# Attention and feed-forward layer on one core: GpSimd takes the residual addition, and four orders of work are changed

## What is computed

```python
attn_out = softmax(q @ k.T / sqrt(32) + mask) @ v @ Wo.T + bo    # 16 heads of 32, keys 0..2047
a = layernorm(x + attn_out) * gamma + beta
x = layernorm(x + a)                              # first output, "x1"
xh = x @ H                                        # Hadamard, 512 x 512
scale = max(|xh|, axis=-1) / 7
xq = clip(round(xh / scale), -8, 7) * scale       # 4 bits
wq = ternary(weight)
x = layernorm(x + xq @ wq.T)                      # the output
```

## Time and profile before

| | |
|---|---|
| time, 3 runs | 4688.91 us median, 4688.58 to 4694.65 |
| profiled execution | 4689.32 us, span 4687.4 us |
| busy share of the span | PE 97%, DVE 71%, ACT 54%, POOL 78% |
| first token stage | 1113.8 to 1273.5 us: 159.7 us, of which PE is busy 143.9, DVE 117.6, POOL 88.2 |
| last token stage | 4539.0 to 4687.4 us |

### The profile page before, as it was taken

One profiled execution on the slowest core, in us unless ns is written; L12 is line 12 of the kernel. 1 busy time (PEld: TensorE's weight loads), 2 busy tenths in 40 slices (PEclk: granted clock), 3 DMA queues, 4 the chain that ended last, 5 costly groups with the idle time before them and its releaser, 6 DMA issues.

```text
span 4687.4 us, 65375 instructions
## 1 busy us (share of the span) xinstructions
PE 4528.7 (97%) x24114; PEld 2416.8 (52%) x24152; DVE 3331.9 (71%) x5886; ACT 2528.7 (54%) x4890; POOL 3642.7 (78%) x1215
## 2 busy tenths in 40 slices
PE   7999999999899999999999999999989999999987
PEld 4545555554555555555454555555545555555434
DVE  5777777677777677777777777776786777777728
ACT  1555555554555555555455555555545555555545
POOL 1788888887488888888758888888865888888885
PEclk9999999999999999999999999999999999999998
DMA  8213333334421333333341233233434123332112
GB/s 174 73 41 73 71 65 71 70 66 111 110 66 41 65 72 70 73 73 74 107 108 42 57 73 69 65 77 62 94 96 111 42 57 62 75 66 62 30 54 75
DMA packets 245776, 344.89 MB, mean 74 GB/s; under 512 B 14801, under 2 KB 100561, under 8 KB 245458
## 3 DMA queue, kind: packets, MB, share of 16 engines
q1 hardware_dynamic: 243282, 339.68, 32.5%
q10 hardware_dynamic: 2176, 1.05, 0.2%
HBM read 205.33 MB, written 33.55 MB: 51 GB/s over the span
## 4 chain that ended last, share of the span: by engine, by line
PE 67%; POOL 20%; DVE 7%; ACT 2%; issue 2%; DMA 2%; SPq 0%; DVEq 0%; POOLq 0%; ACTq 0%
POOL acc L1139 20%; PE ps_m L529 16%; PE ps_s L544 15%; PE ps_o L574 15%; PE ps_z L516 5%; PE ps_z L549 4%; PE ps_z L484 4%; PE ps_m L490 4%; ACT prob L793 1%; PE ps_s L484 1%; PE ps_s L490 1%; PE ps_s L628 1%; DVE prob L1036 1%; DVE ps_m L1026 1%; DVE ps_s L1010 1%
## 5 line engine op out<-in xcount | busy, mean ns | idle before, releaser
L1139 POOL TENSOR_TENSOR acc<-acc,prob 128x2048 f32<-128x2048 f32 x624 | 2859.0, 4582 | 139.3 <-ACT prob L793 65.1
L950 DVE TENSOR_REDUCE umax<-ps_m 128x1 f32<-128x512 f32 x4071 | 2484.6, 683 | 654.3 <-PE ps_m L529 654.3
L793 ACT ACTIVATE prob<-ps_s 128x512 f32<-128x512 f32 x4096 | 2063.6, 625 | 866.8 <-PE ps_s L544 850.5
L529 PE MATMUL ps_m<-kst,qst 97*128 97x512 f32 x4071 | 1722.5, 424 | 8.7 <-DVE umax L950 5.4
L544 PE MATMUL ps_s<-qst,kst 99*128 99x512 f32 x4096 | 1597.2, 411 | 23.6 <-ACT prob L793 18.8
L529 PEld LDWEIGHTS ps_m<-kst,qst 97*128 97x128 f32 x4071 | 768.7, 189 | 579.7 <-DVE umax L950 366.7
L544 PEld LDWEIGHTS ps_s<-qst,kst 99*128 99x128 f32 x4096 | 776.8, 190 | 391.8 <-ACT prob L793 245.2
L574 PE MATMUL ps_o<-prob,vst 128*32 128x512 f32 x8192 | 975.1, 599 | 0.0
L1139 POOL TENSOR_TENSOR acc<-prob 128x2048 f32<-128x2048 f32 x64 | 291.2, 4550 | 322.6 <-ACT prob L793 322.6
L574 PEld LDWEIGHTS ps_o<-prob,vst 128*32 128x32 f32 x8192 | 227.7, 109 | 480.2 <-issue 292.2
L962 DVE RECIPROCAL zinv<-ps_z 128x512 f32<-128x512 f32 x64 | 214.9, 3358 | 272.7 <-PE ps_z L549 272.7
(11 more groups left out here) (123 smaller groups left out, 2558.4 us busy)
## 6 DMA issues: line engine op xcount, KB each, us to landing
xk<-in_xT_dram SPq DMA_DIRECT2D x66, 1024.0 KB, 8.7
xq<-in_xT_dram SPq DMA_DIRECT2D x65, 1024.0 KB, 5.9
kst<-hi SPq DMA_DIRECT2D x128, 256.0 KB, 6.8
qst<-hi SPq DMA_DIRECT2D x128, 256.0 KB, 5.6
wq<-in_wT_dram SPq DMA_DIRECT2D x65, 256.0 KB, 6.2
kst<-lo SPq DMA_DIRECT2D x64, 256.0 KB, 5.6
qst<-lo SPq DMA_DIRECT2D x64, 256.0 KB, 6.8
ctxT_dram<-obuf SPq DMA_DIRECT2D x64, 256.0 KB, 2.4
```

Of the source, the lines that this page charges most:

```text
L529: nc.tensor.matmul(first_banks[u % len(first_banks)] if first else ps_m[:, u % NMB, :], qst[k % 2][0:RSTACK, h, qt * P:(qt + 1) * P], kst[ ...
L793: nc.scalar.activation(prob[:, c % NPB, h, :], ps_s[:, (i * HG * NKC + HG * c + h) % NSB, :], ACT.Exp, scale=SCALE).then_inc(ex, 1)
L950: nc.vector.tensor_reduce(umax[:, m, kb:kb + 1], bank, AX.X, ALU.max).then_inc(mred, 1)
L1139: nc.gpsimd.tensor_tensor(acc[:], a, prob[:, c % NPB], ALU.add).then_inc(padd, 1)
```

## The change

1. **Residual on POOL.** DVE writes the scaled product straight to `tO` in SBUF, and L1032 goes. POOL adds the rows x1 (`residual`) after the butterfly's first half and ahead of its second. The statistics of the second norm are taken ahead of those of the third. PE's waits on `c_fo` become waits on `c_fs`.
2. **Centring in halves.** L1010 becomes two instructions of 256 columns; the first stands ahead of the norms' chain, where DVE waits for ACT's square root.
3. **Keys earlier in the tail.** PE makes a quarter's keys ahead of the step's transposes; ACT and DVE take them in the same step, ahead of rounding and of the scaled product; SP stacks them a step earlier.
4. **Start.** The quarters of stage 1 use slots (0, 1, 1, 0).
5. **Last block.** SP stacks the queries' high parts ahead of the load of the last weights.

The slots of the start, and SP's order in the last block:

```diff
+SECOND = (0, 1, 1, 0)
...
-                    if i == NBLK - 1:
-                        load_last_projection(n)
                     wait_alone(sp, sc, (n + 1) * (HG * NKC), passed)
                     if not (last and i >= NBLK - 2):
                         queries(n + 2, i + 2)
+                    if i == NBLK - 1:
+                        load_last_projection(n)
+                    if not (last and i >= NBLK - 2):
                         low_queries(n + 2, i + 2)
```

PE's program of a token stage, behind the projection of tile s+1 (the call of `keys_of` at the step's end goes):

```diff
+                    t = s - KEY_STEP
+                    if not last and 0 <= t < NQB:
...
+                        keys_of(stage, t, ps_wo[(NT - 3) % 3])
                     t = s - 3
```

ACT's program of a token stage:

```diff
-                    t = s - KEY_STEP - 1
+                    t = s - KEY_STEP
                     if not last and 0 <= t < NQB:
...
                         keys_of(stage, NG + 1, t, ps_wo[(NT - 3) % 3])
+                    t = s - KEY_STEP - 1
+                    if not last and 0 <= t < NQB:
+                        values_of(bb * NG + (NG + 1), NG + 1, t, ps_wo[(NT - 2) % 3])
                     t = s - 3
```

DVE's program of a token stage; `centre(y, half)` is the instruction of L1010 on one half of the columns:

```diff
+                        if 0 <= y < NT:
+                            dve.wait_ge(c_mv, bb * (3 * NT) + moments_by(s))
+                            centre(y, 0)
                         dve.wait_ge(c_sd, bb * (STEPS - 1) + s)
...
                     if 0 <= y < NT:
-                        nc.vector.scalar_tensor_tensor(out=ps_wo[y % 3], in0=ps_wo[y % 3], scalar=mv[:, LN1, 0:1], in1=gam,
-                                                       op0=ALU.subtract, op1=ALU.mult).then_inc(c_ng, 1)
+                        centre(y, 1)
...
-                    k = s - KEY_STEP - 1
+                    k = s - KEY_STEP
...
                     if 0 <= f < NT:
-                        dve.wait_ge(c_ffn, bb * NT + (f + 1))
-                        nc.vector.scalar_tensor_tensor(out=ps_f[f % 2], in0=ps_f[f % 2], scalar=qsc[:, f % 2, 1:2],
-                                                       in1=wscale[:], op0=ALU.mult, op1=ALU.mult).then_inc(c_fs, 1)
-                    if 0 <= f < NT:
...
-                        dve.wait_ge(c_fs, bb * NT + (f + 1))
-                        nc.vector.tensor_tensor(tO[f % NST], ps_f[f % 2], tY[f % 4], ALU.add).then_inc(c_fo, 1)
+                        dve.wait_ge(c_ffn, bb * NT + (f + 1))
+                        nc.vector.scalar_tensor_tensor(out=tO[f % NST], in0=ps_f[f % 2], scalar=qsc[:, f % 2, 1:2],
+                                                       in1=wscale[:], op0=ALU.mult, op1=ALU.mult).then_inc(c_fs, 1)
```

POOL's program of a token stage:

```diff
+                def residual(b, f):
+                    if 0 <= f < NT:
+                        pool.wait_ge(c_fs, b * NT + (f + 1))
+                        nc.gpsimd.tensor_tensor(tO[f % NST], tO[f % NST], tY[f % 4], ALU.add).then_inc(c_fo, 1)
+
...
                     nc.gpsimd.tensor_tensor(tB[:, half:], src[:, 0:half], src[:, half:], ALU.subtract).then_inc(c_bf, 1)
+                    residual(b, t - 2)
                     sv = tB.rearrange("p (a b n) -> p a b n", a=2, b=2)
```

More of the change, by code:

```diff
@@ L294, in stack, with keys_quarter @@
                     sp.dma_start(dst[HD * r:HD * r + HD].bitcast(F32), part.bitcast(F32)).then_inc(done, 16)
-            def keys_quarter(stage, b, s, t):
+            def keys_quarter(stage, b, s, t, slot=None):
+                k = t % 2 if slot is None else slot
                 if t < 2:
@@ L401, in tokens @@
                         store(bb, s - AGE[LN3])
-                    if not last and 0 < s - KEY_STEP <= NQB:
-                        keys_quarter(bb * NG + NG + 1, bb, NG + 1, s - KEY_STEP - 1)
+                    if not last and 0 <= s - KEY_STEP < NQB:
+                        keys_quarter(bb * NG + NG + 1, bb, NG + 1, s - KEY_STEP)
             sp.dma_start(rows[0:1, 8:10, :], band.rearrange("a (b n) -> a b n", b=2)).then_inc(band_ld, 16)
@@ L432, in _ @@
             for t in range(NQB):
-                keys_quarter(1, 0, 1, t)
+                keys_quarter(1, 0, 1, t, SECOND[t])
                 if t == 1:
@@ L631, in tokens @@
                         nc.tensor.matmul(ps_wo[t % 3], ident[:], tXB[t % 2], start=False, stop=True).then_inc(c_wo, 1)
+                    t = s - KEY_STEP
+                    if not last and 0 <= t < NQB:
+                        stage = bb * NG + (NG + 1)
+                        if t == 0:
+                            pe.wait_ge(wkv_ld, (stage + 1) * 32)
+                            pe.wait_ge(c_y, bb * NT + (NT - 2))
+                        else:
+                            pe.wait_ge(k_lo, stage * NQB + t)
+                        keys_of(stage, t, ps_wo[(NT - 3) % 3])
                     t = s - 3
@@ L674, in tokens @@
                         if t == 0:
[L675 to L680, removed]
                             pe.wait_ge(c_y, bb * NT + (NT - 1))
@@ L762, in keys @@
                         act.wait_ge(q_stk, q * NSTK)
+                    k = t % 2 if q is None else SECOND[t]
                     if t >= 2:
-                        act.wait_ge(k_stk[t % 2], stage * (2 * NSTK) + NSTK)
-                    if t == 2 and q is not None:
+                        act.wait_ge(k_stk[k], stage * (2 * NSTK) + NSTK)
+                    if t >= 2 and q is not None and k == 0:
                         act.wait_ge(q_stk, (q + 1) * NSTK)
-                    keys_of(stage, s, t, kbank)
+                    keys_of(stage, s, t, kbank, k)
                     values_of(stage, s, t, vbank)
@@ L805, in attend @@
                         if i == 0:
-                            act.wait_ge(k_stk[0], (stage + 2) * (2 * NSTK))
+                            act.wait_ge(k_stk[1 if n == 0 else 0], (stage + 2) * (2 * NSTK))
                         queries(n + 2, i + 2, ps_z[:, :])
@@ L865, in tokens @@
                         nc.scalar.activation(tHT[t % 2], ps_ht, ACT.Copy).then_inc(c_wtc, 1)
-                    t = s - KEY_STEP - 1
-                    if not last and 0 <= t < NQB:
-                        values_of(bb * NG + (NG + 1), NG + 1, t, ps_wo[(NT - 2) % 3])
             act.sem_inc(oz_cp, 1)
@@ L930, in first_quarter @@
                 dve.wait_ge(k_hi, NQB + t + 1)
-                if t == 2:
+                if t >= 2 and SECOND[t] == 0:
                     dve.wait_ge(q_stk, 2 * NSTK)
                 if t >= 2:
-                    dve.wait_ge(k_stk[t % 2], 2 * NSTK + NSTK)
-                low_part(lo[:, t % 2], hi[:, t % 2], 1, 1, ps_z[:, :]).then_inc(k_lo, 1)
+                    dve.wait_ge(k_stk[SECOND[t]], 2 * NSTK + NSTK)
+                low_part(lo[:, SECOND[t]], hi[:, SECOND[t]], 1, 1, ps_z[:, :]).then_inc(k_lo, 1)
             def maxima(f, i=None, last=False, first=False):
@@ L977, in own, with centre @@
                         dve.wait_ge(c_dve, bb * total + marks[0])
+                    def centre(y, half):
+                        part = slice(half * (D // 2), (half + 1) * (D // 2))
+                        nc.vector.scalar_tensor_tensor(out=ps_wo[y % 3][:, part], in0=ps_wo[y % 3][:, part],
+                                                       scalar=mv[:, LN1, 0:1], in1=gam[:, part],
+                                                       op0=ALU.subtract, op1=ALU.mult).then_inc(c_ng, 1)
                     q, f, y = s - 3, s - 4, s - 1
@@ L1040, in tokens @@
                         mark(nc.vector.bn_stats(stats[:, LN1, :], ps_wo[s % 3]))
+                    if 0 <= y < NT:
+                        dve.wait_ge(c_y, bb * NT + (y + 1))
+                        mark(nc.vector.bn_stats(stats[:, LN2, :], tY[y % 4]))
                     if 0 <= f < NT:
@@ L1172, in tokens @@
                         butterfly(bb, t)
+                    elif t >= NT:
+                        residual(bb, t - 2)
             nc.gpsimd.memset(eps[:], LN_EPS).then_inc(cst_ok, 1)
```

11 lines of the change are left out of this document (4 added, 7 removed).

## The result

The changed kernel takes 4792.95 us (median of 4 runs, 4788.60 to 4797.67), the kernel before 4688.74 beside it (4 runs, 4688.08 to 4694.65). The ratio is 1.022, 95% interval 1.0204 to 1.0236: slower by 2.2%. The profiled span is 4786.7 us, 99.3 more than before.

A forecast was written before the change was run, and what follows sets the result against it. Full steps were taken as bound by nearly equal engine loops, not busy shares; POOL's residual lengthens them. 4689.3 + 41 (full steps) + 48 (three tails) + 4 (last tail) - 5.5 (last block) - 5 (start) gives 4772 us, range 4737 to 4798.

The forecast's parts named there:

- the upper bounds of the terms: Top of the range: full steps 45, tails 54, last tail 4, smaller gains 5, on 4689.3 us; rounded up to 4798.
- the clock: PE's clock falls to its lower level in tail steps 15 to 17: about 1.9 us a step, 4.5 of 5.7 taken.
- Three rings: Full token steps: DVE's program; POOL, PE and ACT (6.95 us); POOL and DVE (7.48); all close near 7.53.
- the third one: Full steps, POOL and DVE: the residual adds 1.03 us, making a step 8.5 us; +41 over four stages.
- the hold: Full steps: DVE's small two-input SBUF instruction waits until POOL's second addition of incoming rows ends.
- the step without hold: Full steps if POOL doesn't delay DVE's small instruction: 7.98 us, from the path through POOL, PE and ACT.
- DVE's freed time: Full steps: removing L1032 and moving half the centring doesn't shorten the step; DVE then waits 2 us per step.
- The tail's knot: Steps 15 to 20, three batches: keys, scaled product, residual and second half wait in a loop, 14.6 us; +16 per batch.
- the link: Tail: DVE makes the keys' low part before the scaled product, so POOL's residual and second half wait; 6 to 8 us.
- Last tail: Last batch, no keys: steps 15 to 18 each take the residual's 1.03 us; +4.
- Last block: Queries stacked sooner, so most of PE's 7.2 us wait for `ctxT` goes; -5.5 (0 to -7).
- Start: Stage 1: ACT's quarter 2 no longer waits for the stacked query; -5, bounds zero and 7.6.

The follow-up runs named there:

- Experiment 1: The kernel before with only the residual moved to POOL, between the butterfly's halves: 4745.9 us, ratio 1.0131.
- experiment 5: The changed kernel with POOL's second addition of incoming rows in two halves, the second after DVE's last scale instruction: 4768.3 us, ratio 1.0167 to the kernel before.
- experiment 2: The changed kernel with the residual's addition back on DVE, the four other parts of the change kept: 4710.4 us, ratio 1.0055 to the kernel before.
- experiment 6: The kernel before with the start's slots, centring in halves and POOL's second addition of incoming rows in halves, the second after DVE's scale instructions: 4668.8 us, ratio 0.996.
- experiment 9: The changed kernel with the keys' low part moved behind the scaled product in DVE's program: 4763.6 us, ratio 1.0159 to the kernel before.
- experiment 8: The kernel before with only SP's changed order in the last block: 4691.3 us, ratio 1.0004.
- experiment 7: The kernel before with only the start's changed slots (0, 1, 1, 0): 4683.8 us, ratio 0.9989.

## Why the prediction was right, and where it was off

The forecast was 4772, the measurement 4793, in the range (4737 to 4798) and on the right side. Its place in the range is in part luck: the upper bounds of the terms (4689.3 + 45 + 54 + 4 - 5) come to 4787, and the last 11 us were added "for the unknown in the clock". The tails' 57.6 lie above their own bound of 54. By its own steps:

- **Three rings, and the third one longer by the residual.** Right: 8.5 us forecast, 8.57 measured, L1008 0.7 long forecast, 0.87 measured, ending with POOL's addition. Experiment 1 shows it with the residual alone, and experiment 5 shows that the hold is the cause of 0.56 us per step. The estimate for the step without hold was 7.98; with 0.14 of hold left, 8.01 was measured. The Trainium skill's rule (SBUF — State Buffer, "Who interferes with whom"), that of a DVE instruction with two SBUF inputs and a GpSimd instruction that reads SBUF the later one waits for the earlier one's end, agrees with the traces in four places here: L1008's like ends 0.02 us after POOL's addition, at 0.87, 0.78, 0.31 and 0.34 long, the last in experiment 2, where it was 0.17 of hold and ate the halved centring.
- **DVE's freed time gives nothing.** Right (DVE busy 74.5 of 93.5). Half of the centring moved into the wait for the square root is worth nothing while the small instruction is held (experiment 2, 7.51 us a step), and 0.2 us a step where the hold is gone (experiment 6, 7.31).
- **The tail's knot.** The mechanism was right but not the whole, and the size off: +16 forecast, +19.2 measured on average. The term that was mis-sized is the clock. I let it fall in two products and part of L651, 1.9 us a step, and took 4.5 of 5.7 for three steps. It also stayed low into the values: L493 4.42 and 4.31 instead of 3.73, 0.6 more per step. With that the step is 14.6 + 1.9 + 0.6 = 17.1, and 17.4 and 17.1 were measured in the first batch. In the second, where the clock came back earlier, 15.9 and 16.4 were measured. I had also thought the knot through POOL to be all of it. It isn't: in the first batch the early keys cost 9.4 by PE and ACT alone (experiment 2), the residual 3.2 alone (experiment 1), and 7.8 of the 20.4 come only when both are there. Over the three tails it is 30.1, 11.2 and 16.3 of 57.6. Cutting the link gave 8.3 back in the first batch (experiment 9), 24.9 in the three.
- **Last tail** +4, measured +4.8. Right.
- **Last block.** The step that failed: "Most of that wait goes ... the gain stays: -5.5". Nothing was gained (experiment 8, ratio 1.0004). The clause "if the stacking delayed it, PE's first projection would be late by the issue of two DMAs" was what happened in the three batches that stack queries there: the weights are issued behind the stacking and land 2.78, 2.76 and 3.30 us after PE could use them. I had called them covered by POOL's sums, though the kernel before already showed waits for them, 0.42 and 0.95 us in two of the three batches, that is, no slack.
- **Start.** -5 forecast, -5.9 for the slots themselves; that the first token stage comes 7.9 sooner has 2.0 in it by which this trace is ahead before the first quarter. So the term was about right. Most of what is missing to the upper bound of 7.6 is in the row of experiment 7: quarter 2 still waits 5.65 us, now for the stacking (`kst<-hi`), where I had put 4.3 for PE's keys. Whether DVE's maxima take any was not tested. With the start alone 5.3 us are left at the end by the span, 5.5 by the medians. The steps 1 to 4 of a token stage vary by up to 4 us from stage to stage with the waits for the loads (19.5 to 23.6 in the kernel before), so a difference of 1 us in one trace can't be placed.

The errors in the gains (about +5), in the three tails (+10) and in the steps and the last tail (+3) are the 17 us by which the spans' difference of 99.3 is above the forecast's 82.5.

## What to carry to other kernels

Moving work from a busy engine to one with a low busy share helps only if its new place isn't on the path that the next step waits for. Before such a move, follow the ring that closes a step on each engine, and mark every small VectorE instruction with two SBUF inputs that may fall into a long GpSimd instruction: its price in these traces is what is left of that instruction. If it falls in, move the GpSimd instruction to another moment (here half an addition; with the halved centring and the start's slots 0.4% faster than the kernel before), rather than shorten VectorE's program. And work put ahead of a short instruction to fill a pause must be checked for what waits behind it on the other engines: the early keys filled one pause of 4 us and made two pauses of 2.0 to 2.7 us in each of three steps.

## What was not expected of the hardware

The hold itself was forecast, from 1.00 us in the earlier trace rows. What the runs add is that an instruction on 128x3 values, 0.17 us alone, is held for the whole rest of POOL's addition beside it, at every length of rest that they offered (0.2 to 0.9 us in the full steps), and ends 0.02 us after it. And PE's clock: in the tail of the changed kernel pauses of 2.0 to 2.7 us, twice a step, stood ahead of L671 and L680 at 1.91 each, and L493 began low too (4.42), where in the full steps the longest pause, 1.5 us ahead of L663, left it at 1.00. The pauses alone don't say when the clock comes back: behind the same 2.23 and 2.48 in step 15, L680 took 1.91 in the first batch and 1.11 in the second.
